# Constants of an attention-and-max kernel made later, and the first transposition cut in two

## The reference

```
h = relu(layernorm(x))                       # over the 256 features
A = adj @ h                                  # W1 = W2 = adj, so C - A is the bias alone
x = x + max over features of relu(A + b0)    # one number per sample and node
h = relu(layernorm(x))
q, k, v = split(h @ w_qkv)                   # 8 heads of 32
attn = softmax(where(adj == 0, -inf, q k^T / sqrt(32)))
o = (attn v) @ w_proj + b_proj
x = x + o + layernorm(o) * gamma + beta
```

## Time and profile before

| | us |
|---|---|
| median of 3 runs | 847.73 (845.4 to 847.89) |
| the profiled execution | 843.2 |
| its span | 841.3 |
| PE busy | 752.9 (89%) |
| DVE busy | 612.7 (73%) |
| ACT busy | 496.4 (59%) |
| POOL busy | 394.3 (47%) |

### The profile page before, as it was taken

The page is one execution under the profiler, slowest core; times in us unless marked ns, Lnnn a source line. Parts: engine busy times, 40 slices in busy tenths (PEclk is TensorE's granted clock), DMA queues, the critical chain, the costliest instruction groups (busy, mean ns, idle before and its releaser), DMA issues.

```text
span 841.3 us, 28575 instructions
## 1 busy us (share of the span) xinstructions
PE 752.9 (89%) x11113; PEld 502.6 (60%) x11113; DVE 612.7 (73%) x1488; ACT 496.4 (59%) x1160; POOL 394.3 (47%) x724
## 2 busy tenths in 40 slices
PE   0668999999999999999999999999999999999662
PEld 0235666666666666666666666666666666666441
DVE  4744677777788877777788777787778887777642
ACT  3234666656666666666666666666666766655440
POOL 5712254554554444444554444554455454443442
PEclk9888999999999999999999999999999999999985
DMA  6355577778876767867767777777786887674321
GB/s 196 75 154 138 134 151 160 150 144 165 165 164 157 165 137 149 158 157 163 175 158 154 166 148 171 143 155 165 167 172 154 165 159 148 127 135 105 58 37 25
DMA packets 167285, 121.36 MB, mean 144 GB/s; under 512 B 83696, under 2 KB 166384, under 8 KB 166640
## 3 DMA queue, kind: packets, MB, share of 16 engines
q1 hardware_dynamic: 67328, 69.72, 31.2%
q10 hardware_dynamic: 82928, 33.04, 21.0%
q0 software_dynamic: 16896, 16.78, 14.3%
HBM read 35.06 MB, written 33.55 MB: 82 GB/s over the span
## 4 chain that ended last, share of the span: by engine, by line
PE 58%; DVE 13%; SPq 10%; issue 9%; DMA 4%; POOL 3%; ACT 3%; ACTq 1%; DVEq 0%; POOLq 0%
PE a_ps L307 13%; SPq L261 10%; DVE smax L655 9%; PE a_ps L320 7%; PE pv_ps L400 7%; PE sc_ps L380 6%; PE sum_ps L403 5%; PE sc_ps L329 5%; PE sum_ps L430 4%; PE sc_ps L352 4%; DMA stack<-pairs 3%; PE a_ps L292 2%; PE pv_ps L415 1%; POOL stack L894 1%; DVE st L688 1%
## 5 line engine op out<-in xcount | busy, mean ns | idle before, releaser
L655 DVE TENSOR_REDUCE smax<-sc_ps 128x4 f32<-128x512 f32 x256 | 164.4, 684 | 26.6 <-PE sc_ps L352 24.7
L647 DVE TENSOR_TENSOR pairs<-a_ps,pairs 128x512 f16<-128x512 f32 x128 | 87.3, 683 | 118.6 <-ACT pairs L543 118.5
L553 ACT ACTIVATE p_sb<-sc_ps 128x512 f32<-128x512 f32 x256 | 146.3, 602 | 41.0 <-PE sum_ps L403 34.3
L816 POOL TENSOR_TENSOR h_parts<-h_sb,h_parts 128x256 f16<-128x256 f32 x128 | 84.3, 670 | 137.0 <-ACT h_parts L507 136.7
L307 PE MATMUL a_ps<-hT,w_hi 128*128 128x512 f16 x512 | 135.6, 388 | 13.8 <-DMA hT<-h_parts 13.8
L822 POOL TENSOR_TENSOR oT_lo<-oT,oT_hi 128x256 f16<-128x256 f32 x128 | 85.6, 669 | 105.6 <-ACT oT_hi L566 105.3
L543 ACT ACTIVATE pairs<-a_ps 128x512 f16<-128x512 f32 x128 | 76.2, 596 | 98.1 <-issue 59.1
L400 PE MATMUL pv_ps<-p_sb,v_sb 128*32 128x128 f32 x2048 | 107.4, 278 | 16.4 <-ACT pv_sb L560 9.8
L850 POOL DMA_DIRECT2D out<-y_sb x32 | 43.1, 1348 | 162.3 <-DVE y_sb L710 162.3
L403 PE MATMUL sum_ps<-p_sb,sel_sum 128*32 128x128 f32 x2048 | 105.7, 273 | 0.0
L352 PE MATMUL sc_ps<-stack 96*128 96x128 f16 x1024 | 84.3, 222 | 11.0 <-DMA stack<-pairs 10.9
(11 more groups left out here) (94 smaller groups left out, 1415.3 us busy)
## 6 DMA issues: line engine op xcount, KB each, us to landing
stack<-pairs SPq DMA_DIRECT2D x768, 64.0 KB, 3.0
out<-in_x SPq DMA_DIRECT2D x32, 512.0 KB, 4.0
out<-y_sb POOLq DMA_DIRECT2D x32, 512.0 KB, 6.6
x_sb<-in_x ACTq DMA_DIRECT2D x31, 512.0 KB, 6.0
stack<-crow SPq DMA_DIRECT2D x64, 8.0 KB, 4.1
w_sb<-in_L_gnn_w_qkv SPq DMA_DIRECT2D x1, 768.0 KB, 5.4
x_sb<-in_x SPq DMA_DIRECT2D x1, 512.0 KB, 4.3
hT<-h_parts ACTq DMA_TRANSPOSE x32, 5.9
```

The costliest lines, as they stand in the source:

```text
L553: nc.scalar.activation(p_sb[:, u % P_SLOTS], sc_ps[u % SC_SLOTS][:], ACT.Exp, scale=SCALE).then_inc(p_ready, 1)
L647: nc.vector.tensor_tensor(pairs[:, 1 - c % 2, c // 2, c % 2], a_ps[c % 2][:], pairs[:, c % 2, c // 2, c % 2], ALU.subtract).then_inc(qklo_ ...
L655: nc.vector.tensor_reduce(smax[:, HC * j:HC * (j + 1), b], sc_ps[u % SC_SLOTS][:], AX.X, ALU.max).then_inc(smax_ready, 1)
L816: nc.gpsimd.tensor_tensor(h_parts[:, par, 1, b], h_sb[:, b], h_parts[:, par, 0, b], ALU.subtract).then_inc(hlo_ready, 1)
```

## The change

Five edits. The adjacency gets a semaphore of its own, and the unused `ident16` goes. The first h is transposed by two DMAs, one for the high and one for the low halves, each issued when its half is complete, both ahead of the load of x(2). The masks' constants stay in the prologue; the other constants of POOL move to the head of turn 1, those of ACT and DVE to the head of turn 2, and PE's waits for them to turns 2 and 3. POOL sets the constant rows of slot 0 only, and SP copies them to slots 1 and 2 by two DMAs at the head of turn 2. Where PE's `transpose_max` and `project_o` took a constant they now take an argument of the same value.

```
@@ -225,7 +227,7 @@
         @block.sync
         def _(sp):
             nc.sync.dma_start(x_sb[:, 0], xg[0]).then_inc(x_loaded, 16)
-            nc.sync.dma_start(adj_sb[:], adj).then_inc(core_load, 16)
+            nc.sync.dma_start(adj_sb[:], adj).then_inc(adj_load, 16)
             nc.sync.dma_start(w_sb[:], w_qkv.rearrange("(c p) n -> p c n", p=P)).then_inc(core_load, 16)
             def step(t, k, a, sc, e, d, prep, norm, load):
+                if t == 2:
+                    sp.wait_ge(ms_rows, 1)
+                    for slot in range(1, SLOTS):
+                        nc.sync.dma_start(stack[STACK:ROWS, slot, 1].rearrange("p h b n -> p (h b n)"),
+                                          stack[STACK:ROWS, 0, 1].rearrange("p h b n -> p (h b n)")).then_inc(ms_copied, 16)
 
         @block.tensor
         def _(pe):
-            pe.wait_ge(core_load, 16 * 2)
+            pe.wait_ge(adj_load, 16)
             pe.wait_ge(pool_const, 1)
             nc.tensor.transpose(sc_ps[0][:, 0, :], adj_sb[:], identf[:]).then_inc(adjT_ps, 1)
-            pe.wait_ge(pool_const, 3)
             pe.wait_ge(act_const, 2)
             pe.wait_ge(dve_const, 3)
             def project_qk(t, par, c):
                 if c == 0:
+                    if t == 0:
+                        pe.wait_ge(hT_first, 16)
                     pe.wait_ge(hT_in, 16 * (t + 1))
...
             def step(t, k, a, sc, e, d, prep, norm, load):
                 if t == 1:
 
-                    pe.wait_ge(pool_const, 7)
-                    pe.wait_ge(act_const, ACT_CONST)
-                    pe.wait_ge(dve_const, DVE_CONST)
-                    pe.wait_ge(ms_rows, SLOTS)
+                    pe.wait_ge(pool_const, 2)
+                    pe.wait_ge(act_const, 3)
+                    pe.wait_ge(dve_const, 5)
                     for way in range(2):
                         for c in range(ROW_TILES):
                             mm = nc.tensor.matmul(sc_ps[1 + way][:, c], ident_rep[:, c].rearrange("p r k -> p (r k)"),
                                                   mask_n[:, way], start=True, stop=True)
                         mm.then_inc(mask_psum, 1)
                     pe.wait_ge(mask_ready, 2)
-                for what in ORDER:
+                if t == 2:
+                    pe.wait_ge(ms_rows, 1)
+                    pe.wait_ge(pool_const, 6)
+                if t == 3:
+                    pe.wait_ge(ms_copied, 16 * (SLOTS - 1))
+                    pe.wait_ge(act_const, ACT_CONST)
+                    pe.wait_ge(dve_const, DVE_CONST)
+                order = ORDER
+                o_before_m = sum(what[0] == "O" for what in order[:order.index("M0")])
+                for what in order:
...
         @block.scalar
         def _(act):
-            act.wait_ge(adjT_ps, 1)
-            nc.scalar.activation(adjT_hi[:], sc_ps[0][:, 0, :], ACT.Copy, scale=WS).then_inc(act_const, 1)
-            act.wait_ge(core_load, 16 * 2)
-            nc.scalar.activation(w_hi[:], w_sb[:], ACT.Copy, scale=WS).then_inc(act_const, 1)
-
-            def later_constants():
-                act.wait_ge(pool_const, 3)
+            def mask_constants():
+                act.wait_ge(pool_const, 2)
                 nc.scalar.activation(ident_rep[:], identb[:].rearrange("p (c k) -> p c k", k=HD).unsqueeze(2).to_broadcast(
                     [P, ROW_TILES, ROW_TILES, HD]), ACT.Copy).then_inc(act_const, 1)
-                act.wait_ge(c_load, 16 * 5)
+
+            def later_constants():
                 nc.scalar.activation(wp_hi[:], wp_sb[:], ACT.Copy, scale=WS).then_inc(act_const, 1)
                 nc.scalar.activation(bp_parts[:, 0], bproj_sb[:], ACT.Copy).then_inc(act_const, 1)
+            def first_transposes():
+                for part, ready in enumerate((hhi_ready, hlo_ready)):
+                    act.wait_ge(ready, G)
+                    nc.scalar.dma_start_transpose(hT[:, 0, part].rearrange("p b c n -> p (b c) n"),
+                                                  h_parts[:, 0, part].rearrange("p b d -> p (b d)")).then_inc(
+                                                      hT_in if part else hT_first, 16)
...
             def step(t, k, a, sc, e, d, prep, norm, load):
                 if t == 1:
                     take_masks()
+                if t == 2:
+                    later_constants()
...
+            act.wait_ge(adjT_ps, 1)
+            nc.scalar.activation(adjT_hi[:], sc_ps[0][:, 0, :], ACT.Copy, scale=WS).then_inc(act_const, 1)
+            act.wait_ge(core_load, 16)
+            nc.scalar.activation(w_hi[:], w_sb[:], ACT.Copy, scale=WS).then_inc(act_const, 1)
             load_x(1, 1)
             for b in range(G):
                 rectify(0, 0, b)
             for b in range(G):
                 h_high(0, 0, b)
+            first_transposes()
+            mask_constants()
             load_x(2, 2)
-            later_constants()
-            transpose_h(0, 0)
+            act.wait_ge(c_load, 16 * 5)
             pipeline(step)
...
             def step(t, k, a, sc, e, d, prep, norm, load):
+                if t == 2:
+                    later_constants()
...
-                dve.wait_ge(core_load, 16 * 2)
+                dve.wait_ge(core_load, 16)
+            def mask_constants():
+                nc.vector.tensor_scalar(mask_n[:, 0], adj_sb[:], 0.0, MASKED, ALU.is_equal, ALU.mult).then_inc(dve_const, 1)
+                nc.vector.tensor_scalar(mask_n[:, 1], sc_ps[0][:, 0, :], 0.0, MASKED, ALU.is_equal,
+                                        ALU.mult).then_inc(dve_const, 1)
+
             def later_constants():
                 nc.vector.memset(bias_ones[:], OS * WS).then_inc(dve_const, 1)
                 nc.vector.memset(bp_rows[:], 0.0).then_inc(dve_const, 1)
-                nc.vector.tensor_scalar(mask_n[:, 0], adj_sb[:], 0.0, MASKED, ALU.is_equal, ALU.mult).then_inc(dve_const, 1)
-                nc.vector.tensor_scalar(mask_n[:, 1], sc_ps[0][:, 0, :], 0.0, MASKED, ALU.is_equal,
-                                        ALU.mult).then_inc(dve_const, 1)
                 dve.wait_ge(c_load, 16 * 5)
                 dve.wait_ge(act_const, 4)
                 nc.vector.scalar_tensor_tensor(wp_lo[:], wp_sb[:], WS, wp_hi[:], ALU.mult,
                                                ALU.subtract).then_inc(dve_const, 1)
-                dve.wait_ge(pool_const, 7)
+                dve.wait_ge(pool_const, 6)
                 nc.vector.tensor_reduce(lo_rows[:], lo_pick[:].rearrange("p h u -> p (h u)"), AX.X,
                                         ALU.add).then_inc(dve_const, 1)
...
             split_core()
             stats_x(1, 1)
             aggregate_x(1)
-            later_constants()
+            mask_constants()
             pipeline(step)
-            for i, m in enumerate((identf, ident16, identb)):
+            for i, m in enumerate((identf, identb)):
+            def later_constants():
+
+                nc.gpsimd.memset(sel_sum[:], 0.0).then_inc(pool_zero, 1)
+                nc.gpsimd.memset(sel_row[:], 0.0).then_inc(pool_zero, 1)
+                nc.gpsimd.memset(lo_pick[:], 0.0).then_inc(pool_zero, 1)
+                pool.wait_ge(pool_zero, 5)
...
+                nc.gpsimd.affine_select(out=lo_pick[:], in_=lo_pick[:], compare_op=ALU.not_equal, fill=-1.0, base=-UNITS,
+                                        pattern=[[-HD, HC], [-1, UNITS]], channel_multiplier=1).then_inc(pool_const, 1)
+
+            def ms_row():
+
+                pool.wait_ge(pool_const, 6)
+                nc.gpsimd.memset(stack[STACK:ROWS, 0, 1], MS).then_inc(ms_rows, 1)
+                pool.wait_ge(ms_rows, 1)
+
             ORDER = ("C0 C1 C2 H0 C3 H1 H2 H3 N0 W0 W1 W2 W3 K0 D0 X0").split()
 
             def step(t, k, a, sc, e, d, prep, norm, load):
+                if t == 1:
+                    later_constants()
+                    ms_row()
+                    pool.wait_ge(c_load, 16 * 5)
...
-            def later_constants():
...
-                pool.wait_ge(pool_const, 7)
-                for par in range(SLOTS):
-                    nc.gpsimd.memset(stack[STACK:ROWS, par, 1], MS).then_inc(ms_rows, 1)
-                    pool.wait_ge(ms_rows, par + 1)
             pool.wait_ge(dve_const, 1)
             invert_std_x(0, 0)
             for b in range(G):
                 h_low(0, 0, b)
-            later_constants()
             invert_std_x(1, 1)
-            pool.wait_ge(c_load, 16 * 5)
             pipeline(step)
             pool.wait_ge(stored, 16 * STEPS)
```

More of the change, by code:

```diff
@@ L92, in build @@
         identf = sb("identf", [P, P])
-        ident16 = sb("ident16", [P, P], F16)
         identb = sb("identb", [P, P], BF16)
@@ L151, in build @@
         core_load = sem("core_load")
+        adj_load = sem("adj_load")
         c_load = sem("c_load")
@@ L164, in build @@
         hT_in = sem("hT_in")
+        hT_first = sem("hT_first")
         a_psum = sem("a_psum")
@@ L205, in build @@
         ms_rows = sem("ms_rows")
```

(44 more changed lines are left out.)

19 lines of the change are left out of this document (9 added, 10 removed).

## The result

| | before | after |
|---|---|---|
| median, first comparison (6 runs each) | 847.36 | 834.5 (831.87 to 838.5) |
| mean of the same runs | 846.4 | 835.1 |
| profiled execution / its span | 843.2 / 841.3 | 831.87 / 830.1 |
| ratio after to before, 95% interval | | 0.9866 (0.9825 to 0.9907) |

The change made the kernel faster, by 1.3%; the interval in us is some 8 to 15. An unedited repetition on another chip (`e12_after_again`) gave 837.16 against 845.44, ratio 0.9896 (0.9867 to 0.9926): 8.3 us. The means lie 11.3 us apart in the first comparison, which is what its ratio says, and 8.6 in the repetition.

A forecast was written before the change was run, and what follows sets the result against it. PE bounds the middle, so only the head counts: SP's issuing from its first copy into stack at 34.55, held by constants and late hT. 9.55 gained less 0.5 is 9.05 off 847.73, 838.7; range 834.9 to 843.5.

The forecast's parts named there:

- (a): Before step 0: the adjacency's own semaphore starts w_hi 0.7 earlier and rectifying at 8.8; 0.45 us gained.
- (b): Before step 0: first h transposed in two DMAs, hT complete at 18.3 (between 16.0 and 21.8); gains 3.1 us.
- (c): Before step 0: x(2) loaded behind the second half, its DVE statistics over at 22.0 to 25.2; only a slow load costs, 1.0.
- (d): Before step 0: constants out of the way, projections 5.3 us, first SP copy at 25.0 for 34.55; 9.55 gained.
- (e): Head of step 1: GpSimd's constants, 9.0 us, hidden in its 11.83 us idle time; cost 0.
- (f): Head of step 2: two SP DMAs copying rows of stack, 0.6 to 0.7 each, hidden in SP's idle time; cost 0.
- (g): Head of step 2: DVE's and ACT's constants, a 3.2 us block, mostly hidden; cost 0.5, bounds 0 and 1.5.
- the forecast's own signs of being wrong: First copy after 28, step 2's S4 released by K1 by over 1 us, or PE's middle busy share under 0.97.
- R1: Head: transposition halves cost like wholes, or ACT's queue holds them; hT at worst 21.8, gain 5.5, 842.2; chance 0.12.
- R3: Step 2: DVE's constants take 14.2 us instead of 3.2, passed one for one to S4; 2.0 slower, 849.7; chance 0.04.
- R4: Head: another wait (x(2)'s statistics, x(1)'s norm) holds the first copy at 33 or later; 846 to 847.7; chance 0.06.
- R2: Step 2: clock and DVE's block together give back 1.5 to 4; 839.7 to 842.2; chance 0.12.

The follow-up runs named there:

- e12_after_again: The changed kernel once more, unedited, on another chip; 837.16 against 845.44, ratio 0.9896.
- e5: Changed kernel with the load of x(2) ahead of the two transpositions on ACT's queue, as before the change; 841.62, ratio 0.9939.
- e8: Changed kernel with, in turn 0 alone, ACT's second high copy before rectifying x(1) and DVE's second subtraction before x(2)'s statistics; 834.31, ratio 0.9891.
- e10: Changed kernel with turn 0's pairs first, x(4) loaded later, x(2)'s load before ACT's constants, ACT's and DVE's constants (except lo_rows) before turn 0; 835.35, ratio 0.9891.
- e4: Kernel before with only the adjacency's own semaphore and the two early transpositions, all constants still in the prologue; 844.45, ratio 0.9974.
- e11: e10 with 6 of the 24 copies into stack issued on ACT's queue in turns 0 and 1; 834.73, ratio 0.988.
- e6: Changed kernel with DVE's constants at the head of turn 1 instead of 2 and ACT's two before turn 0; 836.48, ratio 0.991.
- e1: Changed kernel with h(0) transposed by one DMA again, still ahead of the load of x(2); 837.57, ratio 0.9902.
- e7: Changed kernel with four extra unused DVE subtractions, 7.4 us together, ahead of DVE's constants in turn 2; 840.45, ratio 0.9938.
- e3: Kernel before with only the constants moved; one semaphore for adjacency and weights, one transposition of h(0) behind x(2)'s load; 837.62, ratio 0.9895.
- e9: Changed kernel with ACT's load of x(4) in turn 1 issued later, behind the high part of the row maxima; 838.62, ratio 0.9929.

## Why the prediction was right, and where its sizes were off

The mechanism was right: two causes of 34.55, a late hT and constants that DVE, POOL and ACT had to get through first, with SP's issues behind them. The number was less so. The median lies just below the stated range, and is inside it only when it is measured as a ratio: 0.9866 of the 847.73 from which the forecast started is 836.4. By its steps:

- (a) right: 5.18, 7.12, 8.77 for 5.2, 7.2, 8.8.
- (b) hT at 17.2 for 18.3, in its bounds: a half issued after the first lands in 3.3 us from 13.9, less than the shortest whole (4.4). But the saving was credited too much to the cut: by e5 it is the place on the queue.
- (c) right in kind, missed in weight: PE was ready at 21.4, and DVE's statistics, priced as a case of a slow load only, became the last wait, though x(2) was there and DVE began them as soon as its first subtraction was done. They cost 0.6 in this execution, and hardly anything in the repetition, where PE was ready at 21.65 (e8's copy, without them, is at 23.15, the repetition's at 23.18).
- (d) **the mis-sized term**: the projections took 4.2 for 5.3, as PE's pace went from one level to the other in the middle of them. With hT's 1.1 and the 0.6 given back by (c), that is 9.55 against 11.2. The 1.1 of this step is luck as much as error: the 5.3 came back in e10, with hT as early. The 1.1 of hT is not luck: PE's first projection starts at 17.04 to 17.21 in the repetition, e4, e8, e10 and e11 too.
- (e), (f) right: hidden, 8.7 for 9.0 us of POOL, 1.36 of SP.
- (g) block 3.0 for 3.2 and short casts, as forecast, but its cost 1.2 to 1.4 for 0.5. The wait was wrong: the forecast left S4 of turn 2 to SP's copies, with 0.2 us lost behind them. K1 held it by 1.2 us or more (e6), which is one of the forecast's own signs of being wrong. PE's idle did move ahead of N0 (3.03 us at 63.34), with slow matmuls behind it (two of 512 columns 1.06), as it said. SP's 24 issues were 0.6 longer too. But 11.2 less 0.6 and less this is 9.2 to 9.4, and turn 3 came 10.35 earlier (forecast 9.05): about 1 us comes back between the first copy and turn 3. e6, without the block in turn 2, also gains 0.9 from the mark of turn 1 (10.83) to that of turn 3 (11.73); what it is, is not shown.
- The rest of the 12.9 us between the medians lies behind turn 3, where the forecast had nothing and the repetition (8.3) shows scatter. Between the means it is 1 us (11.3 against 10.35) and in the repetition less than nothing (8.6 against 10.40). In the middle PE was busy 195.06 of 200 us (196.14 before), so that part stayed bound by PE.

R1 fell (hT at 17.2, and e1), R3 fell in its condition and held in its price (e7). R4 fell, though the wait that it named, x(2)'s statistics, did become the last, 10 us earlier than it needed. R2 named the place rightly; what (g) cost is just under its lower end of 1.5.

## What to carry to other kernels

Where two causes hold one instruction, undo both before you judge either: here one was worth 0.4 us alone and 3.7 beside the other. A DMA that waits for another load holds what stands behind it on its queue (e5: 4.1 us); issue first what is ready, and look at what the moved transfer is then next to. To measure a change of 1% in a kernel that scatters as much, compare one instruction of the steady part of the trace, not the whole time, and take a second execution of the same kernel to know how far that instruction scatters itself.

## What the runs showed of the hardware that I had not expected

- The same twelve matmuls of 512 columns from an idle PE took 5.3 us before (0.43 each throughout), 4.2 after, 4.6 in the repetition, 5.3 in e10, though it began within 0.1 us of the changed kernel's start, and 5.3 in e1, where they began at 18.45; in e3 the pace changed in the second group. The granted clock of these stretches reads the same, 1.00, at either pace, in the changed kernel (stretch, its length, busy time of PE with the number of its matmuls, granted clock, DMA share, GB/s):

```profile
17.20:20.00 2.80, 2.77 (x7) 1.00 0.52 180
20.00:21.40 1.40, 1.40 (x6) 1.00 0.00 0
```

  and in e1:

```profile
18.40:21.00 2.60, 2.56 (x7) 1.00 0.55 191
21.00:23.60 2.60, 2.60 (x8) 1.00 0.00 0
```

  Seven matmuls in 2.8 us in one row, six in 1.4 in the next, by the same column. 0.43 us for 512 columns is 1.2 GHz, 0.22 is 2.4. Later the column does follow: around the slow S4 of turn 1 in the changed kernel it reads 0.50.

```profile
44.70:47.00 2.30, 2.23 (x18) 0.50 0.46 153
```

  So for PE's first matmuls the column can't be trusted; the duration of a matmul can. What decides the moment of the change these runs don't show.
- A transposing DMA of 512 KB that went out within 2 us of a 512 KB load ahead of it on ACT's queue was issued in 3.75 to 4.12 us, in all six cases (before, e3, e5 with its two halves, e9, e10, e11). Everywhere else in the 14 traces the issue took 1.3 to 3.84 us, with a median of 2.4.
